# A PSUM copy moved ahead in the filter pass, and two low phases sorted in the 3x3 pass

## The reference

```python
def att(f):                                  # for each of 4 levels
    f_att, f_idt = f[:, :16], f[:, 16:]
    ker = mlp(f_att.mean(axis=(2, 3)))       # one 3x3 kernel per image and channel
    dk = depthwise3x3(f_att, ker)            # the dynamic part
    lk = conv13x13(f_att, lk_filter)         # the fixed large filter
    return conv1x1(concat([lk + dk, f_idt]), fus_w, fus_b)

y0 = conv1x1(relu(conv3x3(gn(x), ds_w3[0])), ds_w1[0])   # level 0, full resolution
# levels 1 to 3: the same at 1/2, 1/4 and 1/8 of the size, repeated up and added
x = x + conv1x1(att(y0) + ups(att(y1)) + ups(att(y2)) + ups(att(y3)), fin_w)
x = x + conv3x3_and_5x5_mixed(gn(x))                     # the second layer
```

## Time and profile before

| | |
|---|---|
| median of 3 runs | 3051.51 us (3051.09 to 3056.02) |
| the profiled execution: its own time, its span | 3052.12 us, 3050.3 us |
| TensorE busy, weight loads | 2688.6 us (88%), 2153.5 us (71%) |
| VectorE, ScalarE, GpSimd busy | 2153.3 us (71%), 992.0 us (33%), 645.2 us (21%) |
| mean granted TensorE clock | 0.940 of full |

### The profile page before, as it was taken

The page is one execution under the profiler, slowest core; times in us unless marked ns, Lnnn a source line. Parts: engine busy times, 40 slices in busy tenths (PEclk is TensorE's granted clock), DMA queues, the critical chain, the costliest instruction groups (busy, mean ns, idle before and its releaser), DMA issues. The chain is left out here.

```text
span 3050.3 us, 39267 instructions
## 1 busy us (share of the span) xinstructions
PE 2688.6 (88%) x12262; PEld 2153.5 (71%) x12262; DVE 2153.3 (71%) x3003; ACT 992.0 (33%) x1606; POOL 645.2 (21%) x732
## 2 busy tenths in 40 slices
PE   0499999996999699999999688888994999999998
PEld 0366776664788678888888566777773777777776
DVE  7444444433345488888888778888876999999998
ACT  1011111110111077778777422222211333232332
POOL 5444433331222143443344200000001000000000
PEclk9999999998889699999999799999996999999999
DMA  4422222210000299999998313333344223333332
GB/s 75 100 71 70 65 71 64 65 42 16 8 13 15 39 199 212 218 215 214 212 217 208 112 59 140 143 127 127 129 151 161 88 88 117 92 113 97 109 103 69
DMA packets 288699, 337.99 MB, mean 111 GB/s; under 512 B 24816, under 2 KB 243824, under 8 KB 274288
## 3 DMA queue, kind: packets, MB, share of 16 engines
q1 hardware_dynamic: 285072, 336.15, 41.2%
q10 hardware_dynamic: 3552, 0.89, 0.1%
HBM read 211.60 MB, written 122.62 MB: 110 GB/s over the span
## 5 line engine op out<-in xcount | busy, mean ns | idle before, releaser
L373 PE MATMUL ps_all<-vh,u_h 128*128 128x512 f32 x960 | 384.7, 401 | 28.7 <-DVE vl L2633 27.8
L375 PE MATMUL ps_all<-vh,u_l 128*128 128x512 f32 x960 | 383.3, 399 | 0.0
L374 PE MATMUL ps_all<-vl,u_h 128*128 128x512 f32 x960 | 382.9, 399 | 0.0
L2542 ACT ACTIVATE vh<-rt,gn 128x528 fp32r<-128x528 f32 x192 | 130.4, 727 | 445.9 <-DVE rt L2610 331.2
L373 PE MATMUL ps_all<-vh,t_h 128*128 128x512 f32 x576 | 231.2, 401 | 22.3 <-DVE vl L1691 22.3
L373 PEld LDWEIGHTS ps_all<-vh,u_h 128*128 128x128 f32 x960 | 180.9, 188 | 82.3 <-issue 35.7
L375 PE MATMUL ps_all<-vh,t_l 128*128 128x512 f32 x576 | 229.7, 399 | 0.0
L374 PE MATMUL ps_all<-vl,t_h 128*128 128x512 f32 x576 | 229.4, 398 | 0.0
L375 PEld LDWEIGHTS ps_all<-vh,u_l 128*128 128x128 f32 x960 | 181.0, 189 | 46.2
L374 PEld LDWEIGHTS ps_all<-vl,u_h 128*128 128x128 f32 x960 | 181.1, 189 | 45.5
L373 PE MATMUL ps_all<-nh,w3h 128*128 128x512 f32 (+1 forms) x396 | 161.0, 407 | 32.3 <-POOL nl L1078 24.5
(11 more groups left out here) (384 smaller groups left out, 6688.6 us busy)
## 6 DMA issues: line engine op xcount, KB each, us to landing
xc<-in_x SPq DMA_DIRECT2D x128, 256.0 KB, 3.8
xr<-in_x SPq DMA_DIRECT2D x128, 256.0 KB, 4.2
x_layer<-xr SPq DMA_DIRECT2D x64, 512.0 KB, 2.7
xq<-x_layer SPq DMA_DIRECT2D x32, 1024.0 KB, 4.8
x_layer<-xq SPq DMA_DIRECT2D x32, 1024.0 KB, 3.8
out<-ot SPq DMA_DIRECT2D x64, 512.0 KB, 5.2
xw<-in_x SPq DMA_DIRECT2D x112, 288.0 KB, 5.0
xw<-x_layer SPq DMA_DIRECT2D x16, 1152.0 KB, 8.7
```

Source lines behind the costliest of these rows:

```text
L373: pe.matmul(o, wh, xh, start=first, stop=False, skip_group_check=True)
L374: pe.matmul(o, wh, xl, start=False, stop=False, skip_group_check=True)
L375: return pe.matmul(o, wl, xh, start=False, stop=last, skip_group_check=True)
L2542: act.activation(vh[:, v % 2, n, :, :].rearrange("p a b -> p (a b)"), rt[:, n, :, :].rearrange("p a b -> p (a b)"), ACT.Identity, scale=gn ...
```

## The change

In the 3x3 pass a new tile `rp_l` holds the low part of r for two of the four phases of the columns (column modulo 4 = 0 and 1), in rows of 36 like `rp_h`. ACT fills it (`low_phases`) from `rl`, one instruction of 128 x 512 elements per tile, between `rp_h` and `features`, behind a wait for DVE's `rl`. Of the four products per tile, dc = 2 and 3 now read `rp_l` instead of `rl`; TensorE waits for it once (semaphore r_p). GpSimd clears the margins of `rp_l` once (two small memsets).

In the filter pass `copy(a, 2)` no longer stands at the head of a period, but `copy(i, 2)` near the end of the one before, ahead of `high_dynamic(n, 2)`.

```diff
@@ 3x3 pass, ACT
+                    def low_phases(i, t):
+                        n = NT * i + t
+                        act.wait_ge(r_l, 1 + n + 1)
+                        v = rl[:, t % 2, :, 2:2 + W].bitcast(F32).rearrange("p n (q d) -> p n q d", d=4)[:, :, :, 0:2]
+                        act.activation(rp_l[:, t % 2, :, :, 1:33].rearrange("p d n q -> p n q d"), v,
+                                       ACT.Identity).then_inc(r_p, 1)
...
                                 high_phases(*later(i, t, 1))
+                                low_phases(*later(i, t, 1))
                             features(i, t)
@@ 3x3 pass, PE
                         for dc in range(4):
+                            if dc == 2:
+                                pe.wait_ge(r_p, n + 1)
                             q0 = dc // 2
                             v = (slice(None), s, (dc + 2) % 4, slice(None), slice(q0, q0 + 34))
                             u = (slice(None), s, slice(None), slice(dc, dc + 133, 4))
+                            low = rl[u] if dc < 2 else rp_l[v]
                             mm = product(pe, ps_fa[:, 0:272].rearrange("p (n q) -> p n q", q=34), fa_h[:, dc, :],
-                                         fa_l[:, dc, :], rp_h[v], rl[u], dc == 0, dc == 3)
+                                         fa_l[:, dc, :], rp_h[v], low, dc == 0, dc == 3)
@@ filter pass, ACT
                     def period(i, a, s, n):
                         first = i is None
-                        if a is not None:
-                            copy(a, 2)
                         if i is not None:
                             high(i, 8, isinstance(i, int) and i == 0)
...
                             high_dynamic(n, 1, first)
                             high(n, 6, first)
                             high(n, 7, first)
+                        if i is not None:
+                            copy(i, 2)
+                        if n is not None:
                             high_dynamic(n, 2, first)
```

More of the change, by code:

```diff
@@ L1438, in conv_kernel @@
             rp_h = sb("rp_h", [P, 2, 4, 8, 36], F32R, stack=st)
+            rp_l = sb("rp_l", [P, 2, 2, 8, 36], F32R, stack=st)
             ft = sb("ft", [P, 4, NPAIR, 9], stack=st)
@@ L1450, in conv_kernel @@
             main, m_c, y_d = sa("main"), sa("m_c"), sa("y_d")
-            r_f, r_h, r_l = sa("r_f"), sa("r_h"), sa("r_l")
+            r_f, r_h, r_l, r_p = sa("r_f"), sa("r_h"), sa("r_l"), sa("r_p")
             q_f, q_x = sa("q_f"), sa("q_x")
@@ L1458, in conv_kernel @@
             w_t3 = Steps(sa("w_t3"), 10)
-            NT3, NFA, NPD = 7, 13, 8
+            NT3, NFA, NPD = 7, 13, 10
             def later(i, t, k):
@@ L1550, in pads @@
                             pool.memset(t[:, :, :, 0:W + 2:W + 1].bitcast(F32), 0.0).then_inc(w_z, 1)
-                        for t in (rp_h,):
+                        for t in (rp_h, rp_l):
                             v = t[:, :, :, :, :].rearrange("p s d n q -> p (s d n) q").bitcast(F32)
@@ L1666, in _ @@
                     high_phases(0, 0)
+                    low_phases(0, 0)
                     with act.Fori(0, B - 1) as i:
```

## The result

The changed kernel takes 3030.99 us, the median of four runs (3025.79 to 3031.58), against 3052.66 us of the kernel before, measured beside it (3051.09 to 3056.02). The ratio is 0.9921 [0.9909, 0.9933]: faster by 0.8%. Forecast were 3032.4 us and a range of 3022 to 3040.5.

What follows compares the result with a forecast made beforehand. TensorE bounds the 3x3 pass; in the filter pass TensorE and VectorE wait for each other in turn. -12.2 - 11.9 + 5.0 = -19.1 us on 3052.12 gives 3033.0, as median 3032.4 us; 8 in 10: 3022 to 3040.5.

Steps and rivals of the forecast that it cites:

- TensorE is the bound of the 3x3 pass, and a matmul on `rl` costs 0.23 us from start to start: 3x3 pass: TensorE busy all 78.00 us; contiguous reads take 0.13 or 0.15 instead, so two per tile save 12.8 us.
- the sum: Whole kernel: -12.2 us in the 3x3 pass, -11.9 in the filter pass, +5.0 for the clock, together -19.1.
- rival (3): 3x3 pass: slow L374 matmul comes from its weights, so `rp_l` changes nothing; 3045.2 us, chance 0.05.
- The new instruction costs 1.1 us and lies beside TensorE's work: 3x3 pass, ScalarE: one fill per tile fits into 1.76 us idle; only the last tile shows about 0.6 us.
- The wait for cc goes, one of 2 us for the aggregate comes, the 5 us wait moves unchanged: Filter pass, TensorE: 2.94 us wait before component 0 vanishes, about 2 us appears before the mean, 4.96 before component 6 stays.
- Rival (2): Filter pass gains nothing, because VectorE holds the whole period and not only the aggregate; 3039.3 us, chance 0.14.
- A loop period gains 2.54 us: Filter pass: component 1 starts 0.30 us behind the aggregate instead of 2.84; four loop periods give -10.2 us.
- The clock takes 5.0 us back: Filter pass: half clock behind six new waits, one chance in two each, 1.65 us per loss; between 0 and +9.9.
- Rival (1): Filter pass: the clock never falls behind the new waits, 5.0 us more gained; 3027.4 us, chance 0.18.

## Why the prediction was right, point by point

**TensorE is the bound of the 3x3 pass, and a matmul on `rl` costs 0.23 us from start to start.** Right. Without the fill the pass got 12.8 us shorter, the figure of the sum; rival (3) falls, since the matmuls on `rp_l` change weights as the old ones did and are followed after 0.13 us.

**The new instruction costs 1.1 us and lies beside TensorE's work.** The price was right (1.19). The cover was thinner than I said. I had set the later `cc` (by 0.97 us) against VectorE's mean idle time of 1.7 us per tile, and not against the moment at which VectorE asks for it. VectorE waits for it, and what it hands to TensorE has less in hand. Where two of VectorE's instructions are also drawn out beside GpSimd, TensorE stalls, about once per image. This is the tile at 1348 (VectorE, GpSimd, TensorE):

```profile
1338.61 2.72 DVE L1726 TENSOR_TENSOR rl<-rf,rh 128x1024 fp32r<-128x1024 f32 x1 [0.38 <-ACT rh L1618]
...
1345.53 2.67 DVE L1701 TENSOR_TENSOR vl<-cr,vh 128x512 fp32r<-128x512 f32 x1
```
```profile
1337.22 3.02 POOL L1544 TENSOR_TENSOR xr<-xr,zr 128x1024 f32<-128x1024 f32 x1
...
1345.48 2.16 POOL L1544 TENSOR_TENSOR xr<-xr,zr 128x1024 f32<-128x1024 f32 x1
```
```profile
1348.33 0.50 PE L373 MATMUL ps_all<-vh,t_h 128*128 128x512 f32 x1 [0.21 <-DVE vl L1701]
```

The `vl` ends at 1348.20, 0.56 us behind the end of GpSimd's instruction (1347.64), and the `rl` at 1341.33, 1.09 behind 1340.24. The shortest `vl` of this form takes 0.68 us and the shortest `rl` 1.21, so each looks like an instruction that got going when GpSimd's was done. Read from start to start, such stalls sum to 3.1 us (ten of them) in the first trace of after and 0.7 with the fill later. That the fill ahead of `cc` makes most of them is shown by moving it; what GpSimd adds is read from these rows alone, as no run moves it. The pass as a whole lost 2.4 us by the fill where the sum had 0.6. In the first trace it lost 1.4 more by the clock, behind a wait that the sum did not look at: -8.7 to -10.4 in place of -12.2.

**The wait for cc goes, one of 2 us for the aggregate comes, the 5 us wait moves unchanged.** Right in all three, at every boundary. The two delays of the aggregate show that it, and not the copy, sets the start of component 1 now. Rival (2), that VectorE holds the whole period, is refuted for this change. It is nearly right two steps further, where VectorE is busy for 92% of the period (244.19 of 266.54 us) and the next copy moved brings nothing.

**A loop period gains 2.54 us.** It gained 3.1 to 3.4, and an outside one 0.9. The step that failed is the one that let the 5 us wait move with all that hangs on it: the wait did, but the half clock began 1.6 us earlier in it, and so 1.7 us less of it was left for the matmuls behind. The periods of the kernel with the copy alone and of that with the mean inside show that the period follows it. What sets where in the wait the half clock begins is open; no run here moves it by itself.

**The clock takes 5.0 us back.** This term failed: behind the six waits that it counts it was 0 in both traces of the changed kernel. I had set one chance in two between a wait of 1.66 without a loss and one of 2.46 with it. Measured ahead of the mean are 1 loss in 35 waits of 2 us, and 5 in 6 of 3 us. At another place, the wait for `xr`, it was 3 in 9 of 2.04 us, and once in three even behind 1.82: the length alone does not decide it. The price per loss was right (a half clock of 3.4 us). The Trainium skill's rule of no gaps over about 3 us ("TensorE: Matmul & The Clock Gate", "Why this matters for your kernels") would have given 0 here, and the delayed aggregate agrees with it. Yet waits of 1.82, 2.04, 2.09, 2.34 and 2.46 us did cost the clock [for the last, rows 9 and 10].

**The sum.** Measured against forecast: 3x3 pass -8.7 to -10.4 for -12.2, what lies behind it -15.3 to -16.7 for -6.9. The two errors have opposite signs, and the stretch ahead of the pass, which no edit moves, differs by a few microseconds more from run to run. So the median came within 1.5 us of the forecast by some luck: the waits and their places were right, both clock terms were not: the one that was counted did not come, and the one that was left out gave 0.6 to 0.9 us a period. Rival (1), without a clock loss, was nearer to what happened; by the chances it was the second.

## What to carry to other kernels

When a wait is taken away, name what the engine meets next and when that is ready; and then look at what hangs behind that second wait on the other engines, since it may be worth more than the first (12.7 us for moving the mean and variance by half a component). Read an operand's price from start to start of the matmuls, not from their durations. An instruction added to an engine with idle time is free only if everything queued behind it on that engine has slack, not just its own result.

The best version is the changed kernel with the mean inside component 1: 3015.47 us, 0.9878 [0.9862, 0.9893] of before. The two further versions (3016.54 with the later fill, 3015.29 with `copy(i, 1)` early as well) can't be told from it.

A microsecond or two between two traces of such a kernel can be the clock alone. Before it is put down to an edit, the granted clock of both has to be looked at, also in stretches that the edit does not touch.

## What the runs showed of the hardware

- A float32r moving operand (the data that a matmul streams) read with a step of 2, 3 or 4 elements costs 1.7 times what it does at step 1: 272 columns take 0.136 us at step 1 and 0.226 to 0.230 at the others. The Trainium skill ("SBUF — State Buffer", in its passage on "cachelines", under "Door 1: The DMA port swizzle") says that lines are 16 bytes, that two hits on a line suffice and that 4 fp32 is as far as one can step for free. At step 2, with two elements on each line, the run contradicts this.
- A VectorE instruction with two operands in SBUF ended about its own length behind the GpSimd instruction beside it (2.67 us where the shortest takes 0.68, and 2.72 for 1.21). The same page, under "SBUF: two separate sides", calls the port that the two share an exclusive lock, held for a whole instruction; the rows above agree with that.
- ScalarE writes 128 x 512 elements sorted into phases in 1.19 us, against 0.60 for the plain copy `cc` (out of PSUM), and with work queued behind it the next instruction starts after 0.97 us (L1636 at 1311.58 in after, the next at 1312.55).
- Behind a wait of about 2 us TensorE's granted clock fell to half in 1 of 35 cases at one place of this program and in 3 of 9 at another; behind one of about 3 us in 5 of 6 (2.99 to 3.12 us) and in 16 of 16 (2.93 to 3.00 us, the kernel before and three kernels with its filter pass). A loss behind a short wait is 3.4 us at half clock.
